# The opening of an attention and feed-forward kernel re-ordered: leading projections, values and first scores

## The reference, cut to what matters

```python
# x: (2, 1024, 512), D=512, H=32 heads, G=8 key/value groups, HD=16, hidden 1376, rank 16
xn = layernorm(x)
q = xn @ Wq                       # 32 heads of 16
k, v = split(xn @ Wkv)            # 8 groups of 16, each shared by 4 heads
s = (softmax(causal(q k^T) / 4) v) @ Wo + bo
gate = xn @ gate_w.T + (xn @ gate_a.T) @ gate_b.T
up   = xn @ up_w.T   + (xn @ up_a.T)   @ up_b.T
hid  = silu(gate) * up
g = silu(hid @ down_w.T + (hid @ down_a.T) @ down_b.T)
out = x + s * g
```

## Time and profile before

| | us |
|---|---|
| median of 3 runs | 985.7 |
| lowest and highest | 982.45 and 990.28 |
| the profiled execution, its own time | 989.02 |
| its span in the profile | 987.3 |
| PE busy in the span | 927.0 (94%) |
| DVE, ACT, POOL busy | 576.7, 487.5, 318.1 |

### The profile page before, as it was taken

One profiled execution on the slowest core, in us unless ns is written; L12 is line 12 of the kernel. 1 busy time (PEld: TensorE's weight loads), 2 busy tenths in 40 slices (PEclk: granted clock), 3 DMA queues, 4 the chain that ended last, 5 costly groups with the idle time before them and its releaser, 6 DMA issues.

```text
span 987.3 us, 18068 instructions
## 1 busy us (share of the span) xinstructions
PE 927.0 (94%) x6599; PEld 598.5 (61%) x6599; DVE 576.7 (58%) x1659; ACT 487.5 (49%) x978; POOL 318.1 (32%) x320
## 2 busy tenths in 40 slices
PE   2797999999999999999999999999999999999986
PEld 2665667676766676767676766554555555555764
DVE  6755666666666666666666666676566656530025
ACT  2432556565656565656565656555444434435211
POOL 4022234343535352525252525330213122120126
PEclk9899999999999999999999999989999999999998
DMA  9456242424242424242424243367565454534454
GB/s 293 132 186 206 64 136 80 133 83 134 82 134 83 133 83 125 86 124 88 119 89 124 93 127 101 101 186 195 166 169 146 124 158 122 139 105 135 144 150 150
DMA packets 142934, 129.02 MB, mean 131 GB/s; under 512 B 36176, under 2 KB 104368, under 8 KB 142624
## 3 DMA queue, kind: packets, MB, share of 16 engines
q1 hardware_dynamic: 142848, 127.87, 43.6%
HBM read 74.07 MB, written 53.22 MB: 129 GB/s over the span
## 4 chain that ended last, share of the span: by engine, by line
PE 84%; DVE 8%; ACT 3%; DMA 2%; issue 2%; POOL 0%; SPq 0%; POOLq 0%; DVEq 0%; ACTq 0%
PE bank L934 24%; PE o L1071 12%; PE bank L246 9%; PE s L1035 9%; PE st L1054 9%; PE bank L247 7%; PE bank L248 7%; DVE junk L1516 2%; PE bank L896 2%; DVE neg_pad L1532 1%; PE bank L909 1%; PE bank L913 1%; DVE hid L1406 1%; DMA inv_sums<-scratch_r 1%; ACT gate L1168 1%
## 5 line engine op out<-in xcount | busy, mean ns | idle before, releaser
L1297 ACT ACTIVATE prob<-st 128x512 f32<-128x512 f32 (+1 forms) x640 | 324.3, 554 | 287.7 <-PE st L1054 287.1
L1516 DVE CUSTOM_DVE_ANT_0 junk<-s,mask 128x128 bf16<-128x128 f32 (+3 forms) x512 | 229.3, 487 | 116.3 <-PE s L1035 115.5
L1519 DVE TENSOR_REDUCE part_max<-s 128x1 f32<-128x512 f32 x256 | 163.8, 681 | 103.9 <-PE s L1035 103.7
L503 POOL TENSOR_SCALAR_AFFINE_SELECT prob<-prob 128x512 f32<-128x512 f32 x128 | 82.3, 655 | 262.1 <-ACT prob L1297 261.6
L1035 PE MATMUL s<-k,q 64*128 64x512 f32 (+3 forms) x768 | 150.0, 379 | 10.5 <-DVE part_max L1516 8.5
L934 PE MATMUL bank<-x_hi,w_hi 64*128 64x512 f32 (+1 forms) x704 | 150.9, 415 | 2.4 <-DVE hid L1406 1.1
L1071 PE MATMUL o<-prob,v 128*32 128x512 f32 (+3 forms) x1536 | 145.3, 497 | 0.0
L934 PE MATMUL bank<-x_lo,w_hi 64*128 64x512 f32 (+1 forms) x704 | 142.9, 391 | 0.0
L934 PE MATMUL bank<-x_hi,w_lo 64*128 64x512 f32 (+1 forms) x704 | 142.2, 389 | 0.0
L1054 PE MATMUL st<-q,k 64*128 64x512 f32 (+3 forms) x768 | 137.2, 375 | 3.9 <-ACT prob L1297 3.8
L512 POOL TENSOR_TENSOR tanh<-tanh,hid 128x512 f32<-128x512 f32 (+1 forms) x44 | 56.5, 1285 | 166.4 <-DVE hid L1406 166.4
(11 more groups left out here) (121 smaller groups left out, 1014.6 us busy)
## 6 DMA issues: line engine op xcount, KB each, us to landing
hid_in<-scratch_hid SPq DMA_DIRECT2D x16, 1408.0 KB, 7.4
q<-scratch_q SPq DMA_DIRECT2D x60, 200.0 KB
scratch_hid<-tanh_hid_hi SPq DMA_DIRECT2D x40, 256.0 KB, 2.1
scratch_hid<-hid_lo SPq DMA_DIRECT2D x40, 256.0 KB, 2.4
scratch_o<-o_sb SPq DMA_DIRECT2D x32, 256.0 KB
scratch_q<-proj_hi SPq DMA_DIRECT2D x30, 256.0 KB
k<-scratch_k SPq DMA_DIRECT2D x30, 192.0 KB
ctx<-scratch_o SPq DMA_DIRECT2D x16, 256.0 KB, 3.9
```

Source lines behind the costliest of these rows:

```text
L503: ins = pool.affine_select(out=blk, in_=blk, compare_op=ALU.is_ge, fill=0.0, base=0, pattern=[[0, REP], [1, P]], channel_multiplier=-1)
L1297: nc.scalar.activation(prob[:, job % 3, h, 0:JOB_COLS[j]], st[at % ST_BANKS][:, 0:JOB_COLS[j]], ACT.Exp, scale=float(HD) ** -0.5).then_inc ...
L1516: ins = dve.tensor_tensor_reduce(junk[:, n % S_BANKS, 0:wd], bank_[:, 0:wd], mask[:, C - wd:C], 1.0, LOWEST, ALU.add, ALU.max, part[:, h, ...
L1519: ins = dve.tensor_reduce(part[:, h, qt, dst:dst + 1], bank_[:, 0:wd], AX.X, ALU.max)
```

## The change

It has five parts.

1. `LEAD` ends after the values of chunks 0 and 1 (32 steps, and `EARLY` falls from 42 to 34), so PE does all eight value steps before any score.
2. The score pairs of the first group are placed over slots 0 to 45 and not over 6 to 45.
3. On ACT, the four leading projections are rounded one after the other as they are filled; `copy_x` of chunk 1, `root(3)` and `split_low_b` come behind them. On DVE, the layernorm of chunk 3 comes behind all four, and `low_of_low` of `low_b` moves behind the keys of chunk 2.
4. For chunks 2 and 3 the order becomes: transposes, keys, values, and the query block of chunk 0 or 1 last, on all engines and in the numbering.
5. `split_low_a` waits only until POOL has taken the low parts of chunk 3; the wait for the stored values moves to ACT's first fold (`split_weight(0, 0)`).

```diff
+FIRST_OF_ALL, FIRST_SLOTS = 0, 45
...
-PROJECTED = LEADING + [p for c in BESIDE for p in (BESIDE[c], (c, KEYS_BLOCK))] + AFTER
+PROJECTED = LEADING + [p for c in BESIDE for p in ((c, KEYS_BLOCK), BESIDE[c])] + AFTER
...
     for c in BESIDE:
         for k in range(KT):
             yield "turn", c, k
-        yield ("proj", *BESIDE[c])
         yield "proj", c, KEYS_BLOCK
         yield "value", c, 0
+        yield ("proj", *BESIDE[c])
...
-LEAD = sum(... if u <= NUMBER["proj", 1, 0])
+LEAD = sum(... if u <= NUMBER["value", 1, 0])
...
-            even = SLOTS * g + FIRST_UNIT + UNIT_SLOTS * sum(weight[:w]) // sum(weight)
+            first, width = (FIRST_UNIT, UNIT_SLOTS) if g else (FIRST_OF_ALL, FIRST_SLOTS)
+            even = SLOTS * g + first + width * sum(weight[:w]) // sum(weight)
...
             def split_low_a():
-                for i in range(2):
-                    act.wait_ge(v_stored[i], DMA * NCH // 2)
-                act.wait_ge(xn_ready, NCH)
+                act.wait_ge(xT_lo_late, 2 * KT)
...
             def split_weight(h, i):
+                if h == 0 and i == 0:
+                    for odd in range(2):
+                        act.wait_ge(v_stored[odd], DMA * NCH // 2)
...
                 for c, blk in LEADING:
-                    if c == 1 and blk == KEYS_BLOCK:
-                        root(3)
-                        split_low_b()
-                        for kt in range(KT):
-                            copy_x(1, kt)
                     yield STEPS["proj"]
                     split_projection(c, blk)
+                for kt in range(KT):
+                    copy_x(1, kt)
+                root(3)
+                split_low_b()
...
                 for c, blk in LEADING:
                     yield STEPS["proj"]
                     low_projection(c, blk)
-                    if (c, blk) == (0, 0):
-                        layernorm(3)
-                low_of_low(0, bT, b_raw, slice(2 * BESIDE_ROWS, 3 * BESIDE_ROWS))
+                layernorm(3)
                 yield 2 * STEPS["value"]
                 for c in BESIDE:
                     yield KT * STEPS["turn"]
                     yield STEPS["proj"]
+                    low_projection(c, KEYS_BLOCK)
+                    if c == 2:
+                        low_of_low(0, bT, b_raw, slice(2 * BESIDE_ROWS, 3 * BESIDE_ROWS))
+                    yield STEPS["value"]
+                    yield STEPS["proj"]
                     low_projection(*BESIDE[c])
-                    yield STEPS["proj"]
-                    low_projection(c, KEYS_BLOCK)
-                    yield STEPS["value"]
```

More of the change, by code:

```diff
@@ L163 @@
 TOTAL = sum(STEPS[kind] for kind, *_ in NUMBER)
-LEAD = sum(STEPS[kind] for (kind, *_), u in NUMBER.items() if u <= NUMBER["proj", 1, 0])
+LEAD = sum(STEPS[kind] for (kind, *_), u in NUMBER.items() if u <= NUMBER["value", 1, 0])
 EARLY = NUMBER_STEPS["fold", 0, 1] - FIRST_HIDDEN - LEAD
@@ L710, in background @@
                     yield STEPS["proj"]
-                    store_projection(*BESIDE[c])
-                    yield STEPS["proj"]
                     store_projection(c, KEYS_BLOCK)
@@ L715, in background @@
                     store_value(c)
+                    yield STEPS["proj"]
+                    store_projection(*BESIDE[c])
                 for c, blk in AFTER[:SOON]:
@@ L990, in background @@
                         yield from turn_x(c, kt)
-                    yield from project(*BESIDE[c])
                     yield from project(c, KEYS_BLOCK)
                     yield from value(c)
+                    yield from project(*BESIDE[c])
                 for c, blk in AFTER[:SOON]:
@@ L1233, in background @@
                     yield STEPS["proj"]
-                    split_projection(*BESIDE[c])
-                    yield STEPS["proj"]
                     split_projection(c, KEYS_BLOCK)
@@ L1238, in background @@
                     copy_value(c)
+                    yield STEPS["proj"]
+                    split_projection(*BESIDE[c])
                 split_low_a()
```

## The result

The changed kernel took 999.32 us (median of 6 runs, 998.4 to 1001.68) against 984.97 us for the kernel before in the same comparison (6 runs). The ratio is 1.0143, with a 95% interval of 1.012 to 1.0165: slower by 14 us, where 3.2 us more and at most 996 had been forecast. The profiled execution after took 998.82 us with a span of 997.0, that of the kernel before 989.02 with a span of 987.3, which is one of its slower ones.

The account below looks back on a forecast made before the run. PE was taken to bound the kernel, through its waits before about 105 us. The terms -3.5 + 3.2 + 3.1 + 3.5 - 8.3 + 1.2 + 4.0 gave +3.2 us on the median of 985.7: 988.9 us, range 981 to 996.

Parts of the forecast that it names:

- What bounds the kernel: PE, busy 927.0 of 987.3 us; what is won or lost before 105 us arrives unchanged at the end.
- A: The lead: values follow the projections at once, first score pair at 49.35 after 2.5 us waiting for its load; -3.5 us.
- B: Keys of chunk 2: without the query block between, they wait for POOL's low parts; +3.2 us.
- C: low_of_low of low_b, behind the keys of chunk 2: it holds up DVE's maxima and PE waits; +3.1 us.
- D: Keys of chunk 3: they wait for POOL's low parts as in B; +3.5 us.
- E: The wait behind low_a: 5.71 us and half of 5.2 us at low clock go, -8.3; +1.2 us stays.
- F: PE's clock falling behind the waits of A to D: two and a half falls of 1.6 us; +4.0 us, bounds 0 and 6.4.
- The rest: Respaced score pairs and EARLY: 0, bounds -0.5 to +0.5 us; group 1's load: 0, at worst +1 us.
- R3: Rival: value stores ahead on SPq delay the load of the second 512 tokens, at worst 9.2 us, 998.1 us; chance 0.09.
- R1: Rival: PE keeps 2.4 GHz through some of the new waits; 982 to 985, say 984 us; chance 0.20.
- R2: Rival: POOL's work and low_of_low stay hidden, so the waits simply go; 973.9 us; chance 0.05.
- R4: Rival: the early split of the leading projections brings nothing, costing at most 1.5 us; 990.4 us; chance 0.06.

Follow-up runs that it names:

- e_wait_only: The kernel before with only split_low_a no longer waiting for the stored values, that wait moved to the first fold; 981.6 us.
- e_order_only: The kernel before with only the new order for chunks 2 and 3 (keys, values, then the query block); 997.7 us.
- e_undo_order: The changed kernel with the order for chunks 2 and 3 taken back to query block, keys, values; 984.8 us.
- e_kept_busy: The changed kernel with 14 or 15 identity transposes in PE's waits ahead of the first score pair and the keys of chunks 2 and 3; 993.3 us.
- e_load_early: The changed kernel with group 1's queries and keys loaded ahead of the store of the last query block; 992.0 us.
- e_all_three: The changed kernel with the edits of e_kept_busy and e_load_early, and low_of_low of low_b behind the layernorm of chunk 3; 987.2 us.

## Why the prediction was wrong

*What bounds the kernel* was read rightly in that PE's waits ahead of the hidden layer decide, and e_wait_only and e_order_only changed the time through them. That the gain "arrives unchanged at the end" did not hold: behind the opening the profiles differ by up to 6 us.

*A* held: the first pair ran at 48.29, forecast 49.35, with 2.25 us of waiting for the load, forecast 2.5.

*B, C, D* held as waits: 2.17 for POOL (forecast 3.2; part of the rest is time that PE spends at the low clock instead), 1.90 + 0.67 behind low_of_low (3.1; the operation took 3.02 us, not 3.88), 3.07 + 0.46 at chunk 3 (3.5). The keys of chunk 2 began 7.1 us after the chunk's first transpose (48.55), those of chunk 3 7.7 us after theirs (77.04), forecast 6.9. A wait of 0.94 us for DVE at 78.64 had not been counted.

*E* held as a wait: 1.18 us left, forecast 1.2.

*F, the clock, is the step that failed.* The prediction wrote "I count two and a half falls of 1.6: +4.0. Bounds: 0, and four falls, 6.4". Five stretches cost 13.1 us. Two things were wrong in it. The length: I had taken some 3.2 us of low clock for each fall, while here it stayed low for 13.3 us, with a second wait inside, and behind the 3.07 us wait for 6.6 us. The longer stretch was in the rows too, 5.2 us of work at 96.6, and was put aside. A second wait is not needed for a long one: in e_order_only it was 10.2 us behind a single wait of 2.77 us. But it may add to one: in e_undo_order, where the wait for the first load (2.09 us) is the same and that for POOL is gone, the clock was low for 3.4 us. What sets the length stays open. And the number: the 1.18 us that E leaves had a fall of its own (104.8 to 108.2), as had the load. e_kept_busy shows the term by taking most of it away without touching the order.

*The rest* failed in its second half: "it lands at about 8 us after that block and its first pair comes at 9.5: 0, at worst +1". It came with 2.81 us of wait and 1.7 us of clock. The prediction doesn't say what its 8 us are made of; PE asked for the load 9.1 us after the block (102.97 to 112.04), near the 9.5 forecast, and it came after 11.9. The only landing that it had measured was 2.3 us, of a load half as large behind an idle queue; here the load stood behind three stores and took 7.4, where the same load elsewhere took 4.0 to 5.2. R3 was just this mechanism, but I applied it to the load of the second 512 tokens, where the measured wait was 0, and not to that of group 1, where part 4 puts stores ahead of a load. e_load_early shows it. (R3 also said that the trace had no load right behind a value store; it had one, of weights, issued at 62.61 behind two of them, which landed after 4.8 us.) The Trainium skill, "DMA: Bandwidth & Descriptors", section on queues, rings and completion order, says that descriptors are consumed in ring order on each DMA engine. The 7.4 us of the load behind stores agree with this; no run here separates order in the ring from the sharing of bandwidth.

With F at 13.1 instead of 4.0 the sum would have been 12.3, and with group 1's wait 15.1. That this is near the 14.4 us of the medians is in part luck, since the sum is one of the opening, and the opening grew by 11.3. Of the 3.8 us too much, A (the first pair a further 1.1 us earlier), B (1.0) and C (0.5) account for 2.6; the other 1.2 stay open. The rivals R1 (the clock holds), R2 and R4 are out. The chances had put 0.11 on slower by over 1%, and its cause in the wrong load.

## What to carry to other kernels

Price a wait of a bound TensorE by what the clock does after it, and price waits together: here two waits of 2.25 and 2.17 us, 7 us apart, cost 9.7 us with their clock (5.3), a single one of 2.77 in e_order_only 7.9 with its own (5.1), and the single one of 4.75 before 6.4 (1.7). So give each fall a range, here 1.7 to 5.1 us, and not one number. Before an independent block is moved from between a producer and its consumer, look for what it covers; here one query block covered 5 us of POOL's work, and taking it away twice brought two waits of 2.7 us and 8 us of low clock behind them. And where a store moves ahead of a load on the same queue, take the landing time from a load of the same size behind stores, not from a smaller one behind an idle queue.

## What the runs showed of the hardware that was not expected

The granted clock fell behind waits of only 2.2 us, and it can fall behind shorter ones. A wait of about 1.2 us for DVE, the one that is left behind low_a, stands in every profile but that of the kernel before, in twelve. In the changed kernel (1.18 us, low from 104.8 to 108.2) and in e_kept_busy (1.19 us at 101.50) 3.4 us at 0.50 followed; in the other ten, e_wait_only among them (1.19 us at 92.75), the clock read 1.00 behind it.

How long it then stays low differs as much: 3.4 us in e_undo_order behind 2.09 us, 6.8 us in the kernel before around the end of its 5.71 us, 10.2 us in e_order_only behind 2.77 us, though PE worked all the time, and 16.9 us in e_load_early (48.1 to 65.0) with the two waits that gave 13.6 us (50.2 to 63.8) in the changed kernel. These runs don't show what decides it.

In e_kept_busy fourteen or fifteen transposes whose result nobody reads, 1.7 to 1.9 us of PE's time, kept the clock at 1.00 through each of three waits and were worth more than they cost. They don't always: with the same transposes in e_all_three it fell at 51.5 all the same, behind waits of 0.93 and 1.60 us.
